# Shared expert units moved ahead of the routed ones in a one-core four-layer kernel

## What is computed

```python
logits = flat @ router_w                                     # flat: 1024 tokens x 256, after a layernorm
scores = jax.nn.softmax(logits, axis=-1)                     # 64 experts
_, topk_idx = jax.lax.top_k(logits + router_bias, K)         # K = 4
topk_scores = jnp.take_along_axis(scores, topk_idx, axis=-1)
topk_scores = topk_scores / topk_scores.sum(axis=-1, keepdims=True)
comb = jnp.zeros((n, E), dtype=flat.dtype).at[jnp.arange(n)[:, None], topk_idx].set(topk_scores)
g = jax.nn.silu(jnp.einsum('nd,edf->nef', flat, wg))
u = jnp.einsum('nd,edf->nef', flat, wu)
routed = jnp.einsum('ne,nef,efd->nd', comb, g * u, wd)
sg = jax.nn.silu(jnp.einsum('nd,sdh->nsh', flat, swg))
su = jnp.einsum('nd,sdh->nsh', flat, swu)
shared = jnp.einsum('nsh,shd->nd', sg * su, swd)
return (routed + shared).reshape(b, t, d)
```

## Time and profile before

| What | Value |
|---|---|
| Time, median of 3 runs | 1189.17 us (1187.58 to 1197.72) |
| Span of the profiled execution | 1187.6 us |
| PE busy | 1014.1 us (85%), 6667 matmuls |
| DVE busy | 732.7 us (62%) |
| ACT busy | 524.5 us (44%) |
| POOL busy | 313.2 us (26%) |
| Gate and up (L802) on the chain that ended last | 16% of the span |
| Down (L828) on that chain | 8% of the span |
| Mean granted clock of PE | 0.914 |

### The profile page before, as it was taken

How to read it: one execution, slowest core, us unless ns; L and a number is a source line. 1 busy time by engine, 2 the same in 40 slices (tenths; PEclk the granted TensorE clock), 3 DMA queues, 4 the chain that set the end, 5 groups by cost and what they waited for, 6 DMA issues and landing times.

```text
span 1187.6 us, 18973 instructions
## 1 busy us (share of the span) xinstructions
PE 1014.1 (85%) x6667; PEld 674.9 (57%) x6669; DVE 732.7 (62%) x1639; ACT 524.5 (44%) x883; POOL 313.2 (26%) x624
## 2 busy tenths in 40 slices
PE   7399999999999888888989899863747978999998
PEld 4278888888887433333456468652314534557566
DVE  6964445444546578768565434797795765783753
ACT  3332222222243777656545441532653644544643
POOL 4024344343346456326333100312203100000000
PEclk9599999999999889988999889965666989999999
DMA  6301211112350000000000300020000000000000
GB/s 146 64 14 44 49 40 47 46 40 53 111 177 1 1 2 3 2 2 3 3 3 4 126 1 1 0 54 1 2 2 1 4 1 0 1 10 2 9 9 9
DMA packets 63068, 32.26 MB, mean 27 GB/s; under 512 B 47696, under 2 KB 61664, under 8 KB 62736
## 3 DMA queue, kind: packets, MB, share of 16 engines
q1 hardware_dynamic: 62992, 31.27, 10.0%
HBM read 29.81 MB, written 1.05 MB: 26 GB/s over the span
## 4 chain that ended last, share of the span: by engine, by line
PE 69%; DVE 20%; ACT 4%; issue 4%; POOL 2%; DMA 1%; POOLq 0%; DVEq 0%; SPq 0%; ACTq 0%
PE bank L802 16%; PE bank L828 8%; PE bank L937 4%; PE bank L1420 3%; PE bank L1226 3%; PE bank L1052 3%; PE bank L1020 2%; PE bank L1155 2%; PE bank L982 2%; PE bank L1206 2%; DVE mx L2418 2%; PE bank L1259 1%; PE bank L1036 1%; DVE mxc L2418 1%; PE bank L1242 1%
## 5 line engine op out<-in xcount | busy, mean ns | idle before, releaser
L2418 DVE TENSOR_REDUCE mx<-bank 128x2 f32<-128x512 f32 (+1 forms) x176 | 117.7, 689 | 72.0 <-PE bank L1155 35.8
L1830 ACT ACTIVATE prob<-bank 128x512 f32<-128x512 f32 x176 | 103.0, 597 | 82.1 <-PE bank L1206 54.7
L1598 ACT ACTIVATE hhi<-hh 128x512 fp32r<-128x512 f32 x72 | 45.5, 632 | 156.3 <-DVE hh L2254 143.1
L2250 DVE TENSOR_TENSOR hu<-bank,sg 128x512 f32<-128x512 f32 x64 | 44.3, 692 | 92.1 <-PE bank L802 92.1
L802 PE MATMUL bank<-xh,wh 128*128 128x512 f32 x288 | 91.4, 398 | 0.3 <-DVE hh L2254 0.3
L802 PE MATMUL bank<-xh,wl 128*128 128x512 f32 x288 | 90.2, 393 | 0.0
L802 PE MATMUL bank<-xlo,wh 128*128 128x512 f32 x288 | 90.1, 394 | 0.0
L2242 DVE TENSOR_TENSOR hlo<-hh,hhi 128x512 fp32r<-128x512 f32 x72 | 57.1, 793 | 50.3 <-ACT hhi L1598 50.3
L2853 POOL TENSOR_TENSOR wl<-wraw,wh 128x512 fp32r<-128x512 f32 x72 | 81.2, 1127 | 13.3 <-POOL wh L2850 13.3
L1676 ACT ACTIVATE sg<-bank 128x512 f32<-128x512 f32 x72 | 43.0, 597 | 64.1 <-PE bank L802 64.1
L2850 POOL CAST wh<-wraw 128x512 fp32r<-128x512 f32 x72 | 37.0, 514 | 101.1 <-issue 51.2
(11 more groups left out here) (486 smaller groups left out, 2246.7 us busy)
## 6 DMA issues: line engine op xcount, KB each, us to landing
wraw<-in_L_ffn_wg_dram SPq DMA_DIRECT2D x64, 64.0 KB, 2.2
wraw<-in_L_ffn_wu_dram SPq DMA_DIRECT2D x64, 64.0 KB, 2.3
wraw<-in_L_ffn_wd_dram SPq DMA_DIRECT2D x32, 128.0 KB, 2.4
l_raw<-in_L_ffn_w_dram SPq DMA_DIRECT2D x2, 1024.0 KB, 6.9
mun<-in_L_ffn_mu_dram SPq DMA_DIRECT2D x1, 2048.0 KB, 7.5
xs<-in_x_dram SPq DMA_DIRECT2D x2, 512.0 KB, 4.5
w1s<-in_L_ffn_W_dram SPq DMA_DIRECT2D x2, 512.0 KB, 8.2
stage<-in_L_ffn_W_in_base_dram SPq DMA_DIRECT2D x1, 1024.0 KB, 8.3
```

What stands on the lines that cost most here:

```text
L1598: return act.activation(dst, src, ACT.Copy, scale=scale)
L1830: act.activation(t.prob[k][:, :], bank[3 + n % 2][:, :], ACT.Exp).then_inc(S("probs"), 1)
L2250: tt(hu[k % 2][:, :], bank[4 + (n + 1) % 4][:, :], sg[k % 2][:, :], ALU.mult).then_inc(once("up_used"), 1)
L2418: V.reduce_max(out_, bank[n % 3][:, :].rearrange("p (h t) -> p h t", h=heads), AX, negate=True)\
```

## The change

The eight shared units become units 0 to 7, and the routed ones 8 to 71. SP loads the shared pairs into the slots first. The router's selection is cut into `ranked` (read the logits, add the bias, row maximum), `chosen` (the four largest) and `combined` (weights and their sum); for half 1, DVE does `chosen` behind the product of unit 0 and `combined` behind that of unit 1. PE turns `comb` behind gate and up of units 3 and 5, into banks 7 and 5 in place of 0 and 1. ACT's copy of it comes behind units 3 and 5, DVE's subtraction too. Layer 2's raw weights are loaded ahead of the loop on SP; ACT sums their absolute values behind units 0 and 1, and the scale is made in unit 6. The six ternary passes stay in the last eight units, which are now routed. The core of the diff:

```diff
             for k in range(SLOTN):
-                load_experts(k, k, None)
+                load_experts(k, None, k)
...
+            stage_load(l2_raw[0], "L2_ffn_w1", D, once("l2_loaded"))
+            stage_load(l2_raw[1], "L2_ffn_w2", F1, once("l2_loaded"))
             with sp.Fori(0, E // 2 // SLOTN - 1) as t:
                 for k in range(SLOTN):
                     sp.wait_ge(once("downs_split"), t * SLOTN + (k + 1))
                     sp.sem_inc(once("went_on"), 1)
-                    load_experts(k, t * SLOTN + (SLOTN + k), None)
-            sp.wait_ge(once("picks"), 2)
-            stage_load(l2_raw[0], "L2_ffn_w1", D, once("l2_loaded"))
-            stage_load(l2_raw[1], "L2_ffn_w2", F1, once("l2_loaded"))
+                    load_experts(k, t * SLOTN + k, None)
...
             pe.wait_ge(S("x_split"), 1)
-            turn_combine(0)
             gate_and_up(0, 0, 0, 0)
             pe.wait_ge(S("x_split"), HALVES)
-            gate_and_up(0, 1, 1, 0, (0,))
-            turn_combine(1)
-            gate_and_up(0, 1, 1, 0, (1,))
-            pe.wait_ge(S("comb_low"), 1)
-            weigh(0, 0, 0, 0)
-            pe.wait_ge(S("comb_low"), HALVES)
-            weigh(0, 1, 1, 0)
-            end_of_batch(pe)
-            gate_and_up(1, 0, 2, 1, (0,))
+            pe.wait_ge(S("router_read"), HALVES)
             for u in range(2 * SLOTN):
...
+                up((u + 1) // 2 % SLOTN, (u + 1) % 2, u + 1, (u + 1) // 2, shared=u + 1 < 2 * SLOTN)
+                if u in (2, 4):
+                    turn_combine(u // 2 - 1)
+                if u == 5:
+                    pe.wait_ge(once("abs_sums"), 2)
+                    mm(bank[4][:, 0:2], ones[:, :], st[:, 0:2], start=True, stop=True).then_inc(once("abs_total"), 1)
                 down(u // 2, u % 2, u, u // 2, first_pair=u < 2)
...
-            gate_silu(0, 0)
-            combine_high(1)
...
-            hidden_rounded(0, 0)
-            for u in range(1, 2 * SLOTN):
+            for u in range(2 * SLOTN):
                 gate(u, u)
+                if u in (3, 5):
+                    combine_high(u // 2 - 1)
+                if u < 2:
+                    if u == 0:
+                        act.wait_ge(once("l2_loaded"), 2 * 16)
+                    act.activation(tern[u][:, :], l2_raw[u][:, :], ACT.Abs, accum_out=st[:, u:u + 1]).then_inc(once("abs_sums"), 1)
...
             tokens_low(0)
+            ranked(0)
             chosen(0)
             tokens_low(1)
-            chosen(1)
-            combine_low(0)
-            combine_low(1)
...
+            combined(0)
+            ranked(1)
...
+            for u in range(2 * SLOTN):
+                shared_hidden(u)
+                if u == 0:
+                    chosen(1)
+                elif u == 1:
+                    combined(1)
+                elif u in (3, 5):
+                    combine_low(u // 2 - 1)
...
+                rest_of_hidden(u % 2, u)
```

More of the change, by code:

```diff
@@ L24 @@
 PAIRS = E // 2 + 4
+COMB_BANKS = (7, 5)
 F1 = 1024
@@ L867, in _ @@
                 if u + 1 < 2 * SLOTN:
[L868 to L871, removed]
+                    up((u + 1) // 2, (u + 1) % 2, T * 8 + u + 1, T * SLOTN + (u + 1) // 2)
                 down(u // 2, u % 2, T * 8 + u, T * SLOTN + u // 2, last_pair=u // 2 == SLOTN - 1)
@@ L1642, in combine_high @@
                 act.wait_ge(S("comb_ps"), h + 1)
-                copy(comb[:, T0 * P * h:T0 * P * (h + 1)], bank[h][:, :]).then_inc(S("comb_high"), 1)
+                copy(comb[:, T0 * P * h:T0 * P * (h + 1)], bank[COMB_BANKS[h]][:, :]).then_inc(S("comb_high"), 1)
             def tokens_high(h):
@@ L1699, in _ @@
             for k in range(2 * SLOTN):
[L1700 to L1703, removed]
                 gate(k, E + k)
@@ L2182, in add_attended0, with ranked @@
                            op0=ALU.mult, op1=ALU.add) for i in range(T0)])
-            def chosen(h):
+            def ranked(h):
                 t = first[h]
@@ L2192, in chosen @@
                 dve.sem_inc(S("router_max"), 1)
+            def chosen(h):
+                t = first[h]
                 step(*[V.max(t.m8[:, i, :], t.lb[:, i, 0:E]) for i in range(T0)])
@@ L2196, in chosen, with combined @@
                 step(tt(t.ct[:, :, :], t.lr[:, :, 0:E], t.lb[:, :, 0:E], ALU.not_equal))
+            def combined(h):
+                t = first[h]
                 dve.wait_ge(S("router_exp"), T0 * (h + 1))
@@ new lines, in _, with routed_hidden @@
+            step = step_once
+            dve.wait_ge(once("picks"), 2)
+            dve.wait_ge(once("rest_loads"), REST * 16)
+            def routed_hidden(k, u):
+                n = 3 * k
+                dve.wait_ge(once("gate_used"), u + 1)
+                dve.wait_ge(once("up_made"), u + 5)
+                tt(hu[k % 2][:, :], bank[4 + (n + 1) % 4][:, :], sg[k % 2][:, :], ALU.mult).then_inc(once("up_used"), 1)
+                dve.wait_ge(once("up_used"), u + 3)
+                dve.wait_ge(once("weight_made"), u - (2 * SLOTN - 1))
+                dve.wait_ge(once("hidden_used"), u + 3)
+                tt(hh[k % 2][:, :], bank[4 + (n + 2) % 4][:, :], hu[k % 2][:, :], ALU.mult).then_inc(once("hidden_full"), 1)
@@ L2269, in _ @@
+            with dve.Fori(1, E // 2 // SLOTN) as t:
+                for k in range(2 * SLOTN):
+                    routed_hidden(k, t * 8 + k)
+                    rest_of_hidden(k, t * 8 + k)
+            for k in range(2 * SLOTN):
+                u = E + k
+                routed_hidden(k, u)
                 rest_of_hidden(k, u)
@@ L2860, in _ @@
             for k in range(SLOTN):
-                split(0, k)
+                split(0, k, shared=True)
             with pool.Fori(1, E // 2 // SLOTN) as t:
@@ L2865, in _ @@
             for k in range(SLOTN):
-                split(E // 2 // SLOTN, k, shared=True)
+                split(E // 2 // SLOTN, k)
             end_loop(3, [n for n in STAGES[2] if n])
```

63 lines of the change are left out of this document (25 added, 38 removed).

## The result

In 20 runs of each the changed kernel takes 1194.74 us (median; 1191.35 to 1201.54), the kernel before 1191.73 (1186.85 to 1199.48): a ratio of 1.0033 with a 95% interval of 1.0016 to 1.0049, so 0.3% slower, 1.9 to 5.8 us. Forecast was 3.6 us more, 1191.2 in the terms of a profiled execution of 1187.6.

What follows compares the result with a forecast made beforehand. PE was taken to bound the units, so time moves only where PE waits: 1187.6 - 0.3 (order) + 1.7 (clock) + 1.4 (late last unit) + 0.8 (clock at the end) = 1191.2 us. Range 1186 to 1196.

Steps and rivals of the forecast that it cites:

- the tail: Last units to last `down`: +1.4 from ternary passes delaying the last unit's `hu`, +0.8 from half clock behind that wait.
- the start: First units on PE: a new 2.2 us wait before the first `down`; -0.3 from reordering, +1.7 from half clock.
- the order: First units: PE as if started at 65.55 against 66.00, -0.45, taken as -0.3 for two new small DVE instructions.
- the clock: Behind the new first wait, PE runs 3.40 us at the 1.2 GHz level: +1.7, bounds 0 and 3.4.
- The named queue: DVE in unit 0: `chosen(1)` stands between `hh(0)` and `hlo(0)`, so PE idles 2.2 us, from 68.9 to 71.1.
- `hlo(0)` reaches PE 0.75 later: Unit 0: DVE free at 70.36, `hlo(0)` at PE by 71.1, using a steady unit's 0.75.
- these exceed 1.48 by 1.1 and 0.2: Last units: passes of 2.62 and 1.66 overrun DVE's 1.48 idle, making the last `hu` about 1.3 late.
- The parts costed at nothing: Layer 2's loads, `comb` turns, ACT's copies and sums, DVE's subtractions: hidden or equal in both orders, 0 us.
- The clock did not stay up: Rival: clock stays up at both new waits, 1188.7 us, or 1187.4 with a short tail; chance 0.26.
- The selection did not leave the path: Rival: first silu need not await half 1's exponentials; 1183.2 us, 1184.6 with the longer tail; chance 0.08.
- Half-clock stretches did not repeat in the shared units: Rival: short PE waits bring several 1.7 us losses; 1196.3 us with four, 1199.7 from six; chance 0.12.
- layer 2's loads were not late: Rival: late loads delay ACT's first sum and `sg(1)`; 5 us late costs about 3, 1194 us; chance 0.02.

Runs made afterwards that it cites:

- PE filled: Changed kernel plus twelve unread matmuls on PE before the first `down`; ratio to the kernel before 1.0011 (0.9991 to 1.0031).
- later split: Changed kernel with POOL's split of pair 2 held until the first `down` is done; one run, first `tokens_low` to last `down` 328.67 us.
- extra pass: Changed kernel plus one DVE pass over 2048 columns in the last unit but one; one run, first `tokens_low` to last `down` 331.37 us.
- `hlo` first: Changed kernel with half 1's `chosen` and `combined` behind `hlo` of units 0 and 1; ratio to the kernel before 1.0001 (0.9976 to 1.0025).
- best: Changed kernel: `ranked(1)` before `combined(0)`, `chosen(1)`, `combined(1)` behind `hlo` of units 0, 1, ternary passes two units earlier; ratio to before 0.9978.
- all pieces behind `hlo`: Changed kernel with `combined(0)`, `chosen(1)`, `combined(1)` behind `hlo` of units 0, 1, 2; ratio to the kernel before 1.0006 (0.9977 to 1.0034).

## Why the prediction was right

**The sum.** It gave +3.6 on the profiled execution; first to last shows +2.5, the timing +1.9 to +5.8. The time lies in the range given and within the 1% that had a chance of 0.92, and the sign was right. But the forecast put the larger part, 2.2 us, at the tail, where 0.2 came, and the smaller, 1.4, at the start, where 2.49 came. One error is 2.0 too much and the other 1.1 too little: that the sum came within 1.1 of first to last is in part luck. The range, too, was set against 1187.6, and over 20 runs the kernel before itself has a median 2.6 above that of its first three, so that 1194.74 lies nearer the upper bound than the change alone would put it.

**The start: mechanism right, size too small.** Forecast was -0.3 for the order and +1.7 for the clock, together +1.4; it is +2.49. With PE filled, about +0.8 is left for the order and 1.5 for the clock: the term of the order had the wrong sign. The named queue is what PE waits for: taking it away gives 3.76 us back, lengthening it by 2.04 costs 2.39. Its size was 3.08 in place of 2.2. The run with the later split takes 0.96 off it, as much as that difference, by taking POOL's split out of `hlo`'s way. The steps that the sum had counted stand where they were expected to within half a microsecond (end of the exponentials 0.2 later, up of unit 1 done at 14.1 behind the mark against 13.6). The failed step is "`hlo(0)` reaches PE 0.75 later": a steady unit's duration was used at a place where POOL starts a split just then, as up of unit 1, done, is what POOL waits for. The Trainium skill ("SBUF — State Buffer", section "Who interferes with whom") has this: a DVE instruction with two inputs in SBUF contends with a GpSimd instruction that reads SBUF, over a shared port that works as an exclusive lock, and the order of issue decides which of the two waits. `hlo` reads `hh` and `hhi` from SBUF; the trace agrees, since it ends 0.55 behind POOL's subtraction (77.29, `hlo` 77.84), a little less than a usual `hlo` later. So does the other direction: the product L2193, which began first (75.73), left POOL's subtraction at 1.47 where 1.30 is usual.

**The clock: right.** The stretch behind the wait ran at the 1.2 GHz level for 3.35 us, as the row of 458.4 had suggested; filling the wait with matmuls took it away and gave 1.50 back (forecast 1.7). In the units of these kernels it fell behind idle stretches of PE of 2.12, 3.06, 3.08, 3.27 and 5.12 us, and stayed up behind 0.55, 1.56, 1.60 and 1.71. The rule of the Trainium skill ("TensorE: Matmul & The Clock Gate", section "Why this matters for your kernels"), by which the term would have been 0, warns only of longer gaps than the 2.2 that was forecast. The wait that came was longer than that, so the kernel with the later split decides: 2.12 us, and the clock fell all the same.

**The tail: mis-sized.** Forecast was +1.4 for a late last unit and +0.8 for the clock; measured +0.2 and nothing. The failed step is "these exceed 1.48 by 1.1 and 0.2": it took the two long passes of before, 2.62 and 1.66, over into a place where they lie differently beside POOL's clears. They are 2.05 and 1.39 now; the excess of the first is 0.6, the second is under 1.48 and adds none, and the 0.2 of the last wait is what is left of it. The clear beside which the fourth pass began, before and after:

```profile
373.18 1.80 POOL L2870 MEMSET kstx<- 128x2048 bf16 x1
```

```profile
380.48 1.80 POOL L2889 MEMSET kstx<- 128x2048 bf16 x1
```

Before, the pass (373.44 to 376.06) ends 1.08 behind the end of that clear (374.98); after, it (381.31 to 383.36) ends 1.08 behind it again (382.28). It is shorter only because it began 0.83 into the clear in place of 0.26. In all ten traces every pass that began beside an instruction of POOL, be it a clear, a copy or a split, ended 1.07 to 1.12 behind that instruction's end, and took 1.21 to 1.28 where it began beside none; an `hlo` that a split or a copy lengthened ended 0.53 to 0.57 behind it, and beside a clear it kept its 0.69. So such a duration is set by what is left of POOL's instruction; it is no property of the pass. The 1.42 that the forecast called uncontended is such a case, too: POOL was at a split (360.40 to 361.11), and the pass ended 1.09 behind it. The links behind it were sound, as the extra pass showed: a lateness of 1.23 there went to the end, with 0.45 on top, and brought the clock down.

**The parts costed at nothing.** In the kernel with `hlo` first, PE has three short waits in its first units, 0.29, 0.55 and, ahead of the second `down`, about 0.2, all on the chain of the products. No wait of PE is on layer 2's loads, ACT's two sums or the turns of `comb`; in the changed kernel ACT's first sum begins at 74.51, straight behind `hhi` (73.98). So these cost PE nothing beyond the turns themselves, as forecast.

**The rivals.** The clock did not stay up. The selection did not leave the path, though it can: best shows 2.0 us of the 4.4 that were bounded. Half-clock stretches did not repeat in the shared units, and layer 2's loads were not late.

## What to carry to other kernels

Work moved off one engine's path has to be looked up in the queue of the engine that does it: here the selection left PE's path and stood in front of the one small product that PE waited for next, so that the order within one unit decided the sign. A wait on PE cost itself and, where the clock fell behind it, another 1.5 us; behind the short waits here, 0.55 to 1.71, it did not fall, so one long wait should cost more than two short ones of the same sum (no run splits a wait in two). And an instruction's duration is to be taken from a row with the same neighbours: the same `hlo` took 0.69 or 1.65, the same two products 0.76 or 2.02, and where a DVE instruction began beside one of POOL's, its end could be reckoned from the end of POOL's.

## What was not expected of the hardware

The time of one execution is set in part ahead of all that was changed. The first `tokens_low` began at 55.3 to 60.8 us in ten executions whose code up to there is the same but for the order of loads. PE's speed makes the larger part of it: the same matmuls of the attention took about twice as long in the changed kernel's execution as in the one before. Before and after:

```profile
24.79 1.91 PE L738 MATMUL bank<-xT,kv 128*64 128x256 f32 x8 [0.79 <-issue]
27.38 1.99 PE L747 MATMUL bank<-kvT,oT 64*128 64x256 f32 x8 [0.68 <-ACT oT L1598]
```

```profile
28.94 3.65 PE L738 MATMUL bank<-xT,kv 128*64 128x256 f32 x8 [0.73 <-issue]
33.27 3.78 PE L747 MATMUL bank<-kvT,oT 64*128 64x256 f32 x8 [0.68 <-ACT oT L1593]
```

This fits the two levels of the clock, but the granted clock does not show it: for the changed kernel it reads 1.00 from the start on, also at 67.08 to 71.20, where two matmuls of 512 columns take 1.05 as against 0.62 just behind. So ahead of the units of that execution I go by the durations.

A part begins with DVE at 7.47: in the changed kernel's execution a tiny instruction took 0.88 us beside POOL's clearing of a strip, and PE waited 0.8 for what stood behind it.

```profile
7.47 0.88 DVE L2065 TENSOR_SCALAR rs<-nw 128x4 int32<-128x4 int32 x1
```

But that does not settle it: with the later split and in the best kernel PE waited the same 0.8 and the mark came at 56.0 and 56.3, and with all pieces behind `hlo` it did not wait and the mark came at 58.06. What decides when PE gets faster there stays open, and was not tried. Behind the units it is the same: from the last `down` to the end took 802.2 to 806.7 us in these ten executions, over code that is the same but for one ternary pass. For a difference of 2 to 3 us in such a kernel, a mark that both traces share is worth more than the spans.
